# GpSimd forms the inverses of the softmax sums itself, with a power of minus one, in place of VectorE's reciprocals

## The chip, the core and the metric

The kernel runs on one core of one Trainium2 chip. The metric is the device time of one launch in microseconds (us), the median of three runs. A core has TensorE (PE in the profile, its weight loads apart as PEld), VectorE (DVE), ScalarE (ACT), GpSimd (POOL) and SyncE (SP, which here only issues DMAs).

## What is computed

A transformer layer in float32: layernorm, attention with 16 heads and a relative position bias, residual; then layernorm and a mixture of 16 experts, of which each token takes four.

```python
q = split_heads(hidden_states @ Wq)      # k and v likewise; B=8, S=512, d_model=128, 16 heads of 64
scores = einsum('bhqd,bhkd->bhqk', q, k) + compute_bias(rel_bias, S, S)
attn = softmax(scores, axis=-1)
ctx = einsum('bhqk,bhkd->bhqd', attn, v)
x = x + ctx.transpose(0, 2, 1, 3).reshape(B, S, -1) @ Wo
topv, topi = top_k(logits(layernorm(x)), 4)
x = x + sum_k softmax(topv)[k] * expert[topi[k]](layernorm(x))
```

## The kernel before

Every engine has its own program, written out by hand, and semaphores tie them together. The attention is a loop over the batch number `b` (0 to 7, 512 tokens each) and, in it, the head pair `i` (0 to 7): 64 steps, here called pairs. Each pair has four visits `v`, one for each 128 rows of queries, and each visit has two heads `hh`, so that a pair has eight score tiles of 128x512.

A tile passes through the engines in this order. TensorE forms the scores (`scores`, L1334, three products of split operands). VectorE adds the bias, writes the tile to `prob` in SBUF, and takes the row's extreme into `nmax` (`scores`, L1040, semaphore `neg_rdy`). ScalarE takes the exponential in place and accumulates the row's sum into `rsum` (`exps`, L884, `exp_rdy`). VectorE inverts the two sums of a visit in one instruction of 128x2 (`reciprocal`, L1046, `rinv_rdy`). GpSimd multiplies both tiles of the visit by the inverses (`normalise_probs`, L816, `norm_rdy`). After that the visits part. Tiles of visits 0 and 1 are transposed in blocks by VectorE (`turn_blocks`, L1062, `tr_rdy`), written to DRAM and read back as `pt_d`, and TensorE weighs the values with them one pair later (`weigh_early`, L1403). Tiles of visits 2 and 3 are transposed by TensorE one pair later (`weights_t`, L1348), copied by ScalarE to `pt_e` (L890) and used by `weigh_late` (L1387). TensorE's order in a pair is: scores of four visits, transposes of the pair before (L1348) with the output projection (L1414) between them, projections of the next pair (L1285 to L1287), `weigh_late`, `weigh_early`.

`weigh_late` waits for `neg_rdy` of the seventh tile of the pair in hand, (3,0), because its bank is shared. On VectorE the tile (3,0) stands behind `turn_blocks(b, i, 0)`, and that waits for `norm_rdy` of visit 0. The order on VectorE is `step` at L1215: four score tiles, reciprocal 0, two tiles, `turn_blocks` 0, tile (3,0), reciprocal 1, tile (3,1), the low parts of the next pair's queries and keys (L1023, L1018), `turn_blocks` 1, reciprocals 2 and 3.

GpSimd's program in the loop (`step` at L819) has, besides the four visits, some work for the routing of the batch before: a power of minus a half on 128x4 for each of the two layernorms (L808, L345), copies, one small multiplication (L348), and the scatters of the routed tokens, one indirect DMA (L372) of 128 rows each, 16 for a batch. They come behind the visits that this table names:

```python
ROUTE_POOL = {(2, 1): ("rstd",), (3, 2): ("copy",), (5, 3): ("weights",)}
SCATTER_AT = [(5, 0), (5, 1)] + [(i, v) for i in (6, 7, 8, 9) for v in range(3)] + [(10, 0), (10, 1)]
LAST_SCATTERS = [(i, v) for i in (5, 6) for v in range(TC)] + [(7, 0)]
```

An `i` of 8 to 10 is pair 0 to 2 of the next batch. So from pair 5 to pair 2 of the next batch the six pairs carry 2, 3, 3, 3, 3 and 2 scatters, in six of the batches; pairs 3 and 4 carry none, and the last batch has four in each of pairs 5 and 6. Ahead of the ninth and the thirteenth scatter of a batch a small copy (L368) is made that the scatter waits for. Behind the attention, the experts' blocks run (L1469 to L1494); the change touches nothing there.

Of the kernel before, what the change touches and what calls it, by code (L numbers as in the profile page):

```python
# [25 lines left out]
ALU = mybir.AluOpType  # L26
# [3 lines left out]
P = 128  # L30
# [7 lines left out]
def layer_kernel(nc, x, wq, wk, wv, wo, rel_bias, onehot, ident, expert_no, before_tok, region, home_row, pad,  # L38
# [17 lines left out]
    TILES = 2 * TC  # L56
    CHUNKS = NPR * TILES
# [28 lines left out]
    with ExitStack() as ctx:  # L86
        def sb(name, shape, dt=F32, stack=ctx):
            return stack.enter_context(nc.sbuf_tensor(name, shape, dt))

        def sem(name):  # L90
            return ctx.enter_context(nc.semaphore(name))
# [2 lines left out]
        x_all = sb("x_all", [P, NCH, D])  # L94
        idn = sb("idn", [P, P])
        minus_half = sb("minus_half", [P, TC])
        stats = sb("stats", [P, 2, TC, 6])
        moments = sb("moments", [P, 2, TC, 2])
        var_eps = sb("var_eps", [P, 2, TC])
# [64 lines left out]
        rsum = sb("rsum", [P, TILES], stack=attn)  # L164
        rinv = sb("rinv", [P, TILES], stack=attn)
# [32 lines left out]
        half_rdy = sem("half_rdy")  # L198
# [4 lines left out]
        s_rdy, neg_rdy, exp_rdy, rinv_rdy, norm_rdy = (sem(n) for n in  # L203
                                                       ("s_rdy", "neg_rdy", "exp_rdy", "rinv_rdy", "norm_rdy"))
# [62 lines left out]
        def pair_after(b, i, k):  # L267

            return divmod(b * NPR + i + k, NPR)
# [35 lines left out]
        def goes_on(b):  # L305

            return b <= LAST
# [490 lines left out]
        def _(pool):  # L798
# [1 line left out]
            pool.memset(done[:], 0.0).then_inc(no_done, 1)  # L800
            pool.memset(ones[:], 1.0).then_inc(one_rdy, 1)
            pool.memset(ones_bf[:], 1.0).then_inc(one_rdy, 1)
            pool.wait_ge(half_rdy, 1)

            def rsqrt(n):

# [2 lines left out]

            def normalise_probs(b, i, v):  # L810

                pool.wait_ge(rinv_rdy, b * VISITS + i * TC + v + 1)
                pool.nop(nofuse=True)
                for hh in range(2):
                    tile = prob[:, v, hh, :]
                    pool.tensor_scalar(tile, tile, rinv[:, 2 * v + hh:2 * v + hh + 1], 1.0, ALU.mult, ALU.mult)\  # L816
                        .then_inc(norm_rdy, 1)
# [192 lines left out]
        def _(dve):  # L1010
# [29 lines left out]
                dve.tensor_tensor_reduce(prob[:, v, hh, :], score_bank(v, hh)[:], strips[:, 2 * i + hh, v * P:v * P + S],  # L1040
                                         -1.0, BIG, ALU.add, ALU.min, nmax[:, n:n + 1]).then_inc(neg_rdy, 1)

            def reciprocal(b, i, v):

                dve.wait_ge(exp_rdy, b * CHUNKS + TILES * i + 2 * v + 2)
                dve.reciprocal(rinv[:, 2 * v:2 * v + 2], rsum[:, 2 * v:2 * v + 2]).then_inc(rinv_rdy, 1)  # L1046

            def turn_blocks(b, i, v):

                if (b, i) == (LAST, NPR - 1):  # L1050
# [59 lines left out]
            def early_extras(b, i):  # L1110

                if i == NPR - 2 and b < LAST:
                    normalise(dve, b + 1, 0, xn, rstd_rdy, xn_rdy)
                if i == 3 and exists(b - 1):
                    route_dve(dve, b - 1, 3)
# [99 lines left out]
            def step(b, i):  # L1215
                up = pair_after(b, i, 1)
                scores(b, i, 0, 0)
                scores(b, i, 0, 1)
                scores(b, i, 1, 0)
                scores(b, i, 1, 1)  # L1220
                reciprocal(b, i, 0)
                scores(b, i, 2, 0)
                scores(b, i, 2, 1)
                turn_blocks(b, i, 0)
                early_extras(b, i)
                scores(b, i, 3, 0)
                reciprocal(b, i, 1)
                scores(b, i, 3, 1)
                extras(b, i)
                if goes_on(up[0]):  # L1230
                    queries_lo(*up, queries_bank)
                    keys_lo(*up, keys_bank)
                if i == NPR - 2 and b < LAST:
                    tokens_lo(b + 1)
                turn_blocks(b, i, 1)
                reciprocal(b, i, 2)
                late_extras(b, i)
                reciprocal(b, i, 3)

            def drain():  # L1240
                turned_lo(0, 0)
# [448 lines left out]
```

## Time and profile before

| what | value |
|---|---|
| device time, median of 3 runs | 1121.62 us (1121.6 to 1124.82) |
| profiled execution, first to last instruction (span) | 1087.2 us |
| device time of the profiled execution by itself | not listed; the median of the runs stands 34.4 us above the span |
| TensorE busy | 1056.9 us, 97% of the span |
| VectorE busy | 834.8 us, 77% |
| ScalarE busy | 839.7 us, 77% |
| GpSimd busy | 685.9 us, 63% |
| mean granted TensorE clock | 0.990 |

"Busy" is the time in which an instruction of that engine was at work. The attention takes about the first 780 us of the span. The page divides the span into 40 slices of 27 us, and in those of the attention, but for the first and the last, GpSimd's share is between 4 and 7 tenths.

### The profile page before, as it was taken

The page shows a single profiled execution, that of the slowest core. Times are in us where ns is not written, and L with a number is a line of the kernel's source. Part 1 is how long each engine was busy: PE and PEld are TensorE (multiplying, and loading weights), DVE is VectorE, ACT ScalarE, POOL GpSimd, SP SyncE. Part 2 cuts the span into 40 slices and gives each one's busy share as a digit, 9 for nine tenths or more (in the row PEclk, how much of TensorE's full clock was granted, in tenths as well). Part 3 has the DMA queues.
Part 4 walks back from the last instruction along what each step waited for, and adds up shares of the span by engine and source line. Part 5 has one row for each costly group of instructions (what it writes and reads, how often), then busy time and mean ns, then how long its engine had stood idle before and what let it go on. Part 6 is the DMA issues. An engine that isn't in the chain of part 4 may idle for free.

```text
span 1087.2 us, 27487 instructions
## 1 busy us (share of the span) xinstructions
PE 1056.9 (97%) x8509; PEld 863.7 (79%) x8510; DVE 834.8 (77%) x2568; ACT 839.7 (77%) x2050; POOL 685.9 (63%) x890
## 2 busy tenths in 40 slices
PE   8999999999999999999999999999799999999993
PEld 4777777777777777777777777777599999999993
DVE  6877888888888978988898888888546444457775
ACT  5888888888888888888888888878667666777661
POOL 4654556774776568477657756665756777655553
PEclk9999999999999999999999999999999999999997
DMA  7676666776676677576757666787722623234552
GB/s 212 177 198 192 194 172 181 206 210 171 207 208 184 179 198 208 165 222 194 201 163 216 194 174 194 207 261 227 252 66 82 158 70 105 79 95 133 162 174 69
DMA packets 135344, 189.09 MB, mean 174 GB/s; under 512 B 19000, under 2 KB 108608, under 8 KB 135216
## 3 DMA queue, kind: packets, MB, share of 16 engines
q1 hardware_dynamic: 126064, 170.65, 55.5%
q0 software_dynamic: 9152, 16.88, 4.6%
q8 instruction: 63, 1.03, 0.4%
q14 instruction: 65, 0.53, 0.2%
HBM read 101.18 MB, written 88.23 MB: 174 GB/s over the span
## 4 chain that ended last, share of the span: by engine, by line
PE 80%; DMA 6%; DVE 5%; issue 4%; POOL 2%; SPq 1%; ACT 1%; DVEq 0%; POOLq 0%; ACTq 0%
PE bank L1334 14%; PE bank L1494 13%; PE bank L1403 9%; PE bank L1348 8%; PE bank L1387 8%; PE bank L1414 4%; PE bank L1481 3%; PE bank L1483 3%; PE bank L1482 3%; PE bank L1285 3%; PE bank L1287 3%; PE bank L1286 3%; DMA pt_d<-pt_dram 3%; DVE shared L1040 2%; DMA pt_dram<-turned 2%
## 5 line engine op out<-in xcount | busy, mean ns | idle before, releaser
L816 POOL TENSOR_SCALAR shared<-shared,rinv 128x512 f32<-128x512 f32 x512 | 351.8, 699 | 224.9 <-DVE rinv L1046 222.9
L884 ACT ACTIVATE shared<-shared,nmax 128x512 f32<-128x512 f32 x512 | 368.4, 733 | 75.8 <-DVE nmax L1040 75.8
L1040 DVE CUSTOM_DVE_ANT_0 shared<-bank,shared 128x512 f32<-128x512 f32 x512 | 330.1, 682 | 77.6 <-issue 33.1
L851 POOL DMA_INDIRECT y_dram<-yb,home x158 | 162.0, 1026 | 94.0 <-issue 47.6
L372 POOL DMA_INDIRECT xs_dram<-copies,slot x128 | 134.8, 1053 | 62.0 <-issue 48.9
L1062 DVE STREAM_TRANSPOSE turned<-shared 128x512 f32<-128x512 f32 x248 | 161.0, 687 | 10.7 <-issue 10.7
L890 ACT ACTIVATE pt_e<-bank 128x512 f32<-128x512 f32 x256 | 145.1, 596 | 18.0 <-PE bank L1348 17.2
L1494 PE MATMUL bank<-shared,act_h 128*128 x1264 | 154.1, 275 | 1.3 <-DVE yb L1188 0.7
L1494 PEld LDWEIGHTS bank<-shared,act_h 128*128 128x128 f32 x1264 | 148.0, 192 | 1.9 <-issue 1.9
L1348 PE MATMUL bank<-idn,shared 128*128 128x128 f32 x1024 | 136.6, 276 | 0.5 <-DVE nmax L1040 0.5
L1348 PEld LDWEIGHTS bank<-idn,shared 128*128 128x128 f32 x1024 | 112.8, 141 | 24.1 <-issue 12.7
L1387 PE MATMUL bank<-pt_e,v_sb 128*64 128x256 f32 x1024 | 124.6, 385 | 3.5 <-DVE nmax L1040 3.0
L916 ACT ACTIVATE act_h<-bank,shared 128x256 f32<-128x256 f32 x316 | 124.2, 476 | 3.4 <-PE bank L1483 3.2
L1403 PE MATMUL bank<-pt_d,v_sb 128*64 128x256 f32 x1008 | 122.7, 385 | 3.8 <-DMA pt_d<-pt_dram 3.5
L1387 PEld LDWEIGHTS bank<-pt_e,v_sb 128*64 128x64 f32 x1024 | 71.1, 136 | 49.2 <-issue 23.6
L1334 PE MATMUL bank<-k_hi,q_lo 64*128 64x512 f32 x512 | 109.1, 421 | 0.9 <-DVE q_lo L1023 0.6
L884 ACT ACTIVATION_READ_ACCUMULATOR shared<-shared,nmax 128x1 f32 x512 | 106.6, 208 | 0.0
L1403 PEld LDWEIGHTS bank<-pt_d,v_sb 128*64 128x64 f32 x1008 | 73.6, 138 | 38.3 <-issue 7.9
L1334 PE MATMUL bank<-k_hi,q_hi 64*128 64x512 f32 x512 | 101.0, 388 | 0.0
L1334 PE MATMUL bank<-k_lo,q_hi 64*128 64x512 f32 x512 | 100.9, 388 | 0.0
L1481 PE MATMUL bank<-xbt_hi,w_lo 128*128 128x256 f32 x316 | 95.6, 303 | 0.0
L1188 DVE TENSOR_TENSOR yb<-bank,shared 128x256 f32<-128x256 f32 x79 | 33.5, 424 | 79.9 <-PE bank L1494 79.9
(162 smaller groups left out, 1886.7 us busy)
## 6 DMA issues: line engine op xcount, KB each, us to landing
pt_dram<-turned SPq DMA_DIRECT2D x496, 128.0 KB
pt_d<-pt_dram SPq DMA_DIRECT2D x124, 512.0 KB
xb<-xs_dram SPq DMA_DIRECT2D x79, 129.0 KB, 2.9
shared<-in_experts SPq DMA_DIRECT2D x16, 514.0 KB
shared<-y_dram SPq DMA_DIRECT2D x32, 256.0 KB, 4.6
shared<-roll_dram SPq DMA_DIRECT2D x4, 768.0 KB, 8.2
y_dram<-yb,home POOLq DMA_INDIRECT x158
xs_dram<-pad_sb SPq DMA_DIRECT2D x17, 129.0 KB, 2.2
```

Of the source, the lines that this page charges most:

```text
L372: pool.indirect_dma_start(xs_dram, bass.IndirectOffsetOnAxis(ap=slot[:, c * TOP + k:c * TOP + k + 1], axis=0), copies[:, c, k % 2, :], Non ...
L816: pool.tensor_scalar(tile, tile, rinv[:, 2 * v + hh:2 * v + hh + 1], 1.0, ALU.mult, ALU.mult)\
L851: pool.indirect_dma_start(y_dram, bass.IndirectOffsetOnAxis(ap=home[:, j, c:c + 1], axis=0), yb[:, j, c, :], None, bounds_check=last_row, ...
L884: act.activation(prob[:, v, hh, :], prob[:, v, hh, :], ACT.Exp, bias=nmax[:, n:n + 1], scale=-1.0, accum_out=rsum[:, n:n + 1]).then_inc(ex ...
L890: act.activation(pt_e[:, hh, :, (v - 2) * P:(v - 1) * P], weights_bank(b, i, v, hh)[:].rearrange("p (j q) -> p j q", j=TC), ACT.Copy)\
L1040: dve.tensor_tensor_reduce(prob[:, v, hh, :], score_bank(v, hh)[:], strips[:, 2 * i + hh, v * P:v * P + S], -1.0, BIG, ALU.add, ALU.min, n ...
L1062: dve.transpose(turned[:, v, :, :, hh, :].rearrange("p k j r -> p j k r"), prob[:, v, hh, :].rearrange("p (j k c) -> p j k c", k=TC, c=BK) ...
L1334: mm = pe.matmul(score_bank(v, hh)[:], q[rows, i % 2, v * P:(v + 1) * P], k[rows, i % 2, :], start=(m == 0), stop=(m == 2))
L1348: mm = pe.transpose(weights_bank(b, i, v, hh)[:, j * P:(j + 1) * P], prob[:, v, hh, j * P:(j + 1) * P], idn[:])
L1387: pe.matmul(ps_a[DH * hh:DH * hh + DH, 2 * P:4 * P], v_sb[:, i // 2 % 2, j, col:col + DH], pt_e[:, hh, j, :], start=(j == 0), stop=(j == T ...
L1403: mm = pe.matmul(ps_a[DH * hh:DH * hh + DH, 0:2 * P], v_sb[:, i // 2 % 2, j, col:col + DH], src[:, :, :, j, hh, :].rearrange("p v a r -> p ...
L1494: mm = pe.matmul(ps_y[:, c * D:(c + 1) * D], act_h[:, q % 2, f, c * P:(c + 1) * P], params[:, bass.ds(w + (W2 + f * D), D)], start=(f == 0 ...
```

## The change

GpSimd no longer waits for VectorE's reciprocal. In each visit it waits for the exponentials of the visit, raises the two sums to the power of minus one, waits for its own result, and normalises as before. VectorE's 256 reciprocals are gone. A tile `minus_one` of 128x2 is set once at the start.

```diff
+        minus_one = sb("minus_one", [P, 2])
...
-            pool.wait_ge(half_rdy, 1)
+            pool.memset(minus_one[:], -1.0).then_inc(half_rdy, 1)
+            pool.wait_ge(half_rdy, 2)
...
             def normalise_probs(b, i, v):
 
+                pool.wait_ge(exp_rdy, b * CHUNKS + TILES * i + 2 * v + 2)
+                pool.nop(nofuse=True)
+                pool.tensor_tensor(rinv[:, 2 * v:2 * v + 2], rsum[:, 2 * v:2 * v + 2], minus_one[:], ALU.pow).then_inc(rinv_rdy, 1)
                 pool.wait_ge(rinv_rdy, b * VISITS + i * TC + v + 1)
                 pool.nop(nofuse=True)
                 for hh in range(2):
...
-            def reciprocal(b, i, v):
-
-                dve.wait_ge(exp_rdy, b * CHUNKS + TILES * i + 2 * v + 2)
-                dve.reciprocal(rinv[:, 2 * v:2 * v + 2], rsum[:, 2 * v:2 * v + 2]).then_inc(rinv_rdy, 1)
-
...
                 scores(b, i, 1, 1)
-                reciprocal(b, i, 0)
                 scores(b, i, 2, 0)
...
                 scores(b, i, 3, 0)
-                reciprocal(b, i, 1)
                 scores(b, i, 3, 1)
...
                 turn_blocks(b, i, 1)
-                reciprocal(b, i, 2)
                 late_extras(b, i)
-                reciprocal(b, i, 3)
```

On GpSimd, in a pair with three scatters (`shared` holds `prob`), the order of instructions before was

```order
L816 TENSOR_SCALAR shared<-shared,rinv 128x512 x4
L368 COPY copies<-home_sb 128x4
L372 DMA xs_dram<-copies,slot 69888x129
L816 TENSOR_SCALAR shared<-shared,rinv 128x512 x2
L372 DMA xs_dram<-copies,slot 69888x129
L816 TENSOR_SCALAR shared<-shared,rinv 128x512 x2
L372 DMA xs_dram<-copies,slot 69888x129
```

and with the change it is

```order
L816 TENSOR_TENSOR rinv<-rsum,minus_one 128x2
L821 TENSOR_SCALAR shared<-shared,rinv 128x512 x2
L816 TENSOR_TENSOR rinv<-rsum,minus_one 128x2
L821 TENSOR_SCALAR shared<-shared,rinv 128x512 x2
L369 COPY copies<-home_sb 128x4
L373 DMA xs_dram<-copies,slot 69888x129
L816 TENSOR_TENSOR rinv<-rsum,minus_one 128x2
L821 TENSOR_SCALAR shared<-shared,rinv 128x512 x2
L373 DMA xs_dram<-copies,slot 69888x129
```

One power stands ahead of every two multiplications; nothing else on GpSimd changed its place, and each power stands behind the scatter of the visit before.

On VectorE, at the end of a pair and the start of the next, the order before, with the semaphores that each waits for, was

```order
L1062 STREAM_TRANSPOSE turned<-shared 128x4x4x32 [waits norm_rdy]
L1046 RECIPROCAL rinv<-rsum 128x2 [waits exp_rdy]
L436 TENSOR_REDUCE esum<-ev 128x4 [waits ev_rdy]
L439 RECIPROCAL einv<-esum 128x4 [waits es_rdy]
L1046 RECIPROCAL rinv<-rsum 128x2 [waits exp_rdy]
L1040 ISA shared,nmax<-bank,shared 128x512 [waits tr_rdy,s_rdy]
```

and with the change it is

```order
L1062 STREAM_TRANSPOSE turned<-shared 128x4x4x32 [waits norm_rdy]
L437 TENSOR_REDUCE esum<-ev 128x4 [waits ev_rdy]
L440 RECIPROCAL einv<-esum 128x4 [waits es_rdy]
L1045 ISA shared,nmax<-bank,shared 128x512 [waits tr_rdy,s_rdy]
```

The reciprocals of visits 2 and 3 stood behind the transposes of visit 1; with the change nothing of VectorE stands between ScalarE's sums and GpSimd.

## Rows read from the trace of the kernel before

**Rows 1.** The page, its first part: busy us (share of the span) xinstructions.

```profile
PE 1056.9 (97%) x8509; PEld 863.7 (79%) x8510; DVE 834.8 (77%) x2568; ACT 839.7 (77%) x2050; POOL 685.9 (63%) x890
```

**Rows 2.** Windows: us, busy of PE, PEld, DVE, ACT, POOL, clock, DMA share, GB/s.

```profile
454.84:525.12 70.28, 70.14 (x558) 53.58 (x556) 59.95 (x188) 59.69 (x146) 51.40 (x68) 1.00 0.71 204
479.00:525.12 46.12, 46.12 (x370) 35.18 (x368) 38.72 (x121) 39.40 (x96) 35.57 (x47) 1.00 0.74 213
525.12:550.44 25.32, 25.19 (x204) 19.17 (x203) 22.23 (x74) 20.18 (x49) 12.57 (x19) 1.00 0.60 167
743.44:768.58 25.14, 23.46 (x188) 18.14 (x186) 19.79 (x62) 19.79 (x49) 18.25 (x24) 1.00 0.78 233
```

**Rows 3.** Waits: engine line <- releaser: us in total, times, longest us.

```profile
POOL shared L816 <- DVE rinv L1046: 222.9, 149, 4.5
```

**Rows 4.** Timeline of TensorE, pair 1 of batch 4: start, us, engine, line.

```profile
406.51 0.50 PE L1334 MATMUL bank<-k_hi,q_lo 64*128 64x512 f32 x2
...
414.41 1.95 PE L1387 MATMUL bank<-pt_e,v_sb 128*64 128x256 f32 x16
...
418.01 0.50 PE L1334 MATMUL bank<-k_hi,q_lo 64*128 64x512 f32 x2
```

**Rows 5.** Timeline of VectorE, the same pair.

```profile
411.95 1.30 DVE L1062 STREAM_TRANSPOSE turned<-shared 128x512 f32<-128x512 f32 x2
413.18 0.65 DVE L1040 CUSTOM_DVE_ANT_0 shared<-bank,shared 128x512 f32<-128x512 f32 x1
```

**Rows 6.** Timeline of GpSimd, the same pair.

```profile
407.11 1.37 POOL L816 TENSOR_SCALAR shared<-shared,rinv 128x512 f32<-128x512 f32 x2 [1.93 <-DVE rinv L1046]
408.65 1.05 POOL L372 DMA_INDIRECT xs_dram<-copies,slot  x1 [0.17 <-issue]
409.74 2.70 POOL L816 TENSOR_SCALAR shared<-shared,rinv 128x512 f32<-128x512 f32 x4
```

**Rows 7.** Timeline of ScalarE: the sums of tiles (2,1), (3,1), then (0,1).

```profile
404.73 0.24 ACT L884 ACTIVATION_READ_ACCUMULATOR shared<-shared,nmax 128x1 f32 x1
...
406.14 0.23 ACT L884 ACTIVATION_READ_ACCUMULATOR shared<-shared,nmax 128x1 f32 x1
...
409.67 0.19 ACT L884 ACTIVATION_READ_ACCUMULATOR shared<-shared,nmax 128x1 f32 x1
```

**Rows 8.** Groups of instructions: xcount | busy us, mean ns of one | idle before.

```profile
L345 POOL TENSOR_TENSOR rstd<-var_eps,minus_half 128x4 f32<-128x4 f32 x8 | 8.4, 1056 | 0.8 <-DVE var_eps L387 0.6
L808 POOL TENSOR_TENSOR rstd<-var_eps,minus_half 128x4 f32<-128x4 f32 x8 | 8.2, 1024 | 4.6 <-DVE var_eps L387 4.6
L368 POOL COPY copies<-home_sb 128x4 f32<-128x4 f32 x16 | 3.1, 191 | 0.0
L348 POOL TENSOR_TENSOR wt<-ev,einv 128x16 f32<-128x16 f32 x8 | 1.7, 212 | 0.0
L1046 DVE RECIPROCAL rinv<-rsum 128x2 f32<-128x2 f32 x256 | 36.4, 148 | 0.3
```

**Rows 9.** Timeline: hand-overs to GpSimd from a result just made.

```profile
425.27 0.17 DVE L1046 RECIPROCAL rinv<-rsum 128x2 f32<-128x2 f32 x1
...
425.61 0.69 POOL L816 TENSOR_SCALAR shared<-shared,rinv 128x512 f32<-128x512 f32 x1 [1.00 <-DVE rinv L1046]
...
496.82 1.06 POOL L372 DMA_INDIRECT xs_dram<-copies,slot  x1 [0.78 <-POOL copies L368]
...
1030.93 0.42 DVE L1188 TENSOR_TENSOR yb<-bank,shared 128x256 f32<-128x256 f32 x1 [0.43 <-PE bank L1494]
...
1032.10 0.97 POOL L851 DMA_INDIRECT y_dram<-yb,home  x1 [1.09 <-DVE yb L1188]
```

**Rows 10.** Timeline, last batch, pair 6, four scatters: GpSimd, VectorE, TensorE.

```profile
762.10 1.37 POOL L816 TENSOR_SCALAR shared<-shared,rinv 128x512 f32<-128x512 f32 x2
...
762.88 1.33 DVE L1062 STREAM_TRANSPOSE turned<-shared 128x512 f32<-128x512 f32 x2 [1.96 <-issue]
...
764.95 1.95 PE L1387 MATMUL bank<-pt_e,v_sb 128*64 128x256 f32 x16 [1.45 <-DVE nmax L1040]
```

## The prediction

> **What bounds the kernel now.** The page's first part comes first [rows 1]: TensorE is busy for 97% of the span, GpSimd for 63%. By these shares GpSimd has room to spare. The shares are averages over stages, though, and the change puts work on GpSimd in the attention alone, so I looked there by windows [rows 2]. The first row is a stretch from pair 5 of batch 4 to pair 2 of batch 5, from the start of one pair's scores on TensorE to another's: six pairs in 70.28 us, with the 16 scatters of a batch. TensorE is busy for 70.14 of it at full granted clock (1.00), so it sets the pace: some 11.5 us for a pair, as from 406.51 to 418.01 [rows 4]. GpSimd is busy for 51.40. The row from 525.12 is the two pairs without scatters behind it: GpSimd is busy for 12.57 of 25.32. So GpSimd's load is uneven, and what the change costs must be read in the stretches with scatters.
>
> The view of waits then shows GpSimd idle for 222.9 us, in 149 waits for VectorE's inverse [rows 3]. It reads like a loss that the change takes back. It is mostly spare time: the engine that sets the pace doesn't wait for it.
>
> **Whether a late GpSimd is felt.** The normalised tiles of visit 0 are wanted first. In the pair of [rows 4 to 6] GpSimd normalises the last visit of the pair before and visit 0 from 409.74 to 412.44 without a break; VectorE transposes from 411.95 to 413.25, scores tile (3,0) from 413.18 to 413.83, and TensorE starts `weigh_late`, which waits for that tile, at 414.41. That leaves 0.5 us. The last batch shows what happens beyond it [rows 10]: in a pair with four scatters the normalising of visit 0 starts only at 762.10, VectorE idles 1.96 us before its transposes, and TensorE then idles 1.45 us, its wait put down to VectorE. The window from 743.44, two such pairs, has TensorE busy for only 23.46 of 25.14 us [rows 2]. So where GpSimd's work for a pair is longer than the pair, the pair grows to GpSimd's time. This limit exists already, and the change loads the engine that has it.
>
> **What goes.** 256 reciprocals of 148 ns [rows 8], 36.4 us of VectorE's time. VectorE is busy for 59.95 of 70.28 us in the stretch and TensorE hardly waits for it, so I set this at nothing; a gain is bounded by the 0.14 us in which TensorE is idle in the stretch. The wait also goes in which GpSimd's work on visits 2 and 3 stood behind VectorE's transposes of visit 1: tile (2,1) was summed at 404.97, tile (3,1) at 406.37 [rows 7], and GpSimd started at 407.11 after 1.93 us idle [rows 6]. It can now start at 405. This is real, and it is why I may count GpSimd as a queue that runs without holes when it is late.
>
> **What comes.** In each of 256 visits a power of 128x2 and a wait of GpSimd for its own result. Call their sum x.
>
> The trace has no power of 128x2. One of 128x4 takes 1.02 to 1.06 us, while a copy of the same 128x4 takes 0.19 [rows 8]. So the power itself adds 0.83. If that goes by elements, two columns cost 0.19 + 0.42 = 0.6 us; if it goes by the instruction, 1.02. These are my inner bounds. The outer one below is 0.2, that of any small instruction: a multiplication of 128x16 takes 0.21. I take 0.6: that multiplication with four times the columns costs the same as the copy, so what the power adds seems to be work done per element and not per instruction. The row can't prove it.
>
> The wait: VectorE's reciprocal ends at 425.44 and GpSimd starts at 425.61, 0.17 us later [rows 9]. A scatter behind a copy starts 0.78 us after it, which would be 0.6 more; but a scatter behind VectorE's result (ended 1031.35, started 1032.10) also takes 0.75, so the extra belongs to the indirect DMA and not to waiting for oneself. I take 0.15 and keep 0.78 as the bound above.
>
> So x is 0.75, by the other reading of the power 1.17; the ends are 0.35 and 1.8 (1.02 and 0.78).
>
> **The sum.** First the point from which it decides. In the stretch GpSimd is busy for 51.40 us; beside it stand 14 gaps of 0.17 before scatters [rows 6] and two of 0.78 behind copies [rows 9], 3.9 us. 70.3 less 55.3 leaves 15.0 us for 24 visits: x up to 0.62 fits. In the two pairs behind, 8 visits have 25.32 - 12.57 = 12.7 us, 1.6 a visit, so they are hit only near the upper end.
>
> By pairs, at x = 0.75: two normalisings take 1.35 (2.70 for four), and with a scatter behind them 2.63 (407.11 to 409.74) [rows 6]; a visit then takes 2.10 or 3.38. Pair 5 needs 11.2 us and pair 6 12.2, which fits. Pair 7 needs 12.2, pairs 0 and 1 need 13.0 each (with the small copy and its gap, 0.8), pair 2 12.0 (with a power of 1.02). Together 50.3 us, where there are now 46.12, the row from 479.00 to 525.12 [rows 2]: 4.2 over. GpSimd may be late by some 1.0 us first: visit 0's sums are ready at 409.86 [rows 7], so its tiles can be done at 411.96 instead of 412.44, and there was 0.5 us left. So 3.2 us for each stretch, and there are six: 19. The two pairs with four scatters need 8 x 3.38 + 0.2 = 27.2 us against 25.14: 2.1 over, less 1.0, makes 1. The first pair, where all wait for the first tiles, 0.5. At the end of the attention visits 2 and 3 are released sooner; nothing. Sum: 20.5 us on the 1087.2 of the profiled execution. The median of the runs is 34.4 us above that span, outside of what the profile shows, and I leave this part as it is: 1121.6 + 20.5 = **1142**.
>
> The memset and the tile `minus_one` cost 0.1 us while the input loads; nothing.
>
> **The rivals.**
>
> *The power is cheap: no change.* x = 0.35. GpSimd needs 55.3 + 8.4 = 63.7 of 70.28 us in the stretch; no pair without four scatters is late. In the pairs with four, 27.2 - 3.2 = 24.0 of 25.14 us are needed, and visits 2 and 3 start sooner, so that up to the 1.45 us of [rows 10] comes back in each. 1119 to 1122. For it: the reciprocal on VectorE is as cheap as that, and small instructions cost 0.2. Against it: both powers in the trace cost five times that. It decides from x below 0.65. Chance 0.14, of which 0.03 for over 0.3% faster.
>
> *The power costs by the instruction.* x = 1.17; visits take 2.52 and 3.80 us. Pairs 5 to 2 then need 12.8, 13.9, 13.9, 14.7, 14.7 and 13.7, together 83.7 against 70.3: 13.4 over, less 0.5 that may be late, 13.0; six make 78. The pairs with four scatters add 5, the start 1: 84 us, 1206. For it: the same 1.02 in all 16 powers, with no second size. Against it: the argument on the elements above. Values of x between the two lie between 1142 and 1206. Chance 0.28, with these.
>
> *The wait for oneself is dear.* With 0.78 and a power of 1.02, a visit takes 3.15 without a scatter, four of them 12.6 us, over the 11.5 us of every pair. Each stretch gives 13.4 + 24 x 0.61 = 28, the six 168, and the other 28 pairs about 1 each: some 200 us, 1320. With a power of 0.6 x is 1.38 and the time about 1240. Chance 0.05.
>
> **How the numbers follow.** The forecast, slower by GpSimd's excess at x near 0.75, has 0.53, with 1128 to 1158 as its own range (x 0.68 to 0.85). The range leaves out the cheap power and the dear wait, 0.19 in all, and reaches from the lower end of the forecast to just above the costly power: 1127 to 1209. A measurement of this kernel can tell about 0.3%, 3.4 us, from no change. Faster 0.03, same 0.12, slower 0.85.
>
> **What would show it.** In the profile of the changed kernel the power of 128x2 stands in a row of its own: about 0.6 us if right. GpSimd's busy time rises by 256 times that, about 154 us, to some 840, and VectorE's falls by 36. Pairs with scatters are longer than 11.5 us, those from 7 to 2 most; VectorE waits for GpSimd's tiles before its transposes (L1062), and TensorE for VectorE before `weigh_late` (L1387). Pairs 3 and 4 keep their 25.3 us. The prediction is wrong in size if the power's row says 1.0, wrong in kind if pairs without scatters grow too, and wrong in sign if the six pairs still take 70.3 us.

## The result, and the profile after

The changed kernel takes 1201.07 us (median of 4 runs, 1198.94 to 1207.33) against 1121.61 for the kernel before (4 runs, 1119.62 to 1124.82): a ratio of 1.0703 [1.0679, 1.0728], 79.5 us more. The forecast of 1142 had the direction right and the size wrong by a factor of four; the time lies inside the range, which reaches up to the 1206 us of the dear power, a rival that did not come true.

Of the changed kernel, the page's first part and, from the groups of instructions of GpSimd, the three that matter (busy us, mean ns | idle before):

```profile
PE 1096.0 (91%) x8509; PEld 887.3 (74%) x8510; DVE 822.9 (69%) x2312; ACT 844.0 (70%) x2050; POOL 885.0 (74%) x1147
```

```profile
L821 POOL TENSOR_SCALAR shared<-shared,rinv 128x512 f32<-128x512 f32 x512 | 349.7, 694 | 44.5 <-POOL rinv L816 44.5
L816 POOL TENSOR_TENSOR rinv<-rsum,minus_one 128x2 f32<-128x2 f32 x256 | 184.5, 721 | 80.9 <-ACT shared L889 77.5
L373 POOL DMA_INDIRECT xs_dram<-copies,slot x128 | 139.7, 1091 | 58.8 <-issue 47.7
```

The power costs 0.72 us and the wait for it 44.5 / 256 = 0.17. So x is 0.89, where the prediction took 0.75. GpSimd's busy time rose by 199 us [rows 1], the 222.9 us of waits for VectorE's inverses [rows 3] are gone, and TensorE went from 97% busy to 91% (96% in a second trace of the kernel before, which is used from here on; its span is 1120.6 us).

The chain that ended last, by engine, says who sets the pace now. TensorE had 80% of it in the first trace of the kernel before, GpSimd 2%.

```profile
PE 50%; POOL 25%; issue 12%; ACT 4%; DVE 4%; DMA 3%; another core or an unknown queue 0%; SPq 0%; POOLq 0%; DVEq 0%; ACTq 0%
```

The stretch of [rows 2] again, at its times in this trace, and the two pairs behind it (windows: us, busy of PE, PEld, DVE, ACT, POOL, clock, DMA share, GB/s):

```profile
497.80:577.06 79.26, 72.28 (x560) 55.30 (x558) 58.80 (x162) 60.21 (x146) 66.71 (x90) 1.00 0.66 180
577.06:604.42 27.36, 25.32 (x204) 19.11 (x203) 23.01 (x68) 20.29 (x49) 20.47 (x31) 1.00 0.57 157
```

70.28 became 79.26, and the two pairs that were to keep their 25.3 us became 27.36. A pair's period is the time from the start of its scores on TensorE to the start of the next pair's. Periods in us in batch 5, pairs 5 to 7, and batch 6, pairs 0 to 4 (before: the second trace):

| pair | 5 | 6 | 7 | 0 | 1 | 2 | 3 | 4 |
|---|---|---|---|---|---|---|---|---|
| before | 11.50 | 12.31 | 12.07 | 11.50 | 11.51 | 11.51 | 13.25 | 12.07 |
| after | 11.50 | 15.67 | 11.77 | 12.94 | 13.69 | 13.69 | 17.16 | 11.92 |

Summed over all: the six stretches from pair 5 to pair 2 give 51.4 us, pairs 3 and 4 of seven batches 21.0, the pairs up to batch 1's pair 2 give 4.8, and pairs 5 and 6 of the last batch 5.3. That is 82.5 in the attention (753.8 to 836.3 from the first scores to the last pair's), and the rest of the span is 2.7 shorter.

**Pairs 1 and 2: GpSimd is the bound.** GpSimd in pair 1 of the same stretch, a queue without holes but for the fixed short ones in brackets:

```profile
549.10 1.10 POOL L373 DMA_INDIRECT xs_dram<-copies,slot  x1 [0.18 <-issue]
550.24 0.73 POOL L816 TENSOR_TENSOR rinv<-rsum,minus_one 128x2 f32<-128x2 f32 x1
551.14 1.36 POOL L821 TENSOR_SCALAR shared<-shared,rinv 128x512 f32<-128x512 f32 x2 [0.17 <-POOL rinv L816]
552.68 1.10 POOL L373 DMA_INDIRECT xs_dram<-copies,slot  x1 [0.18 <-issue]
...
561.80 0.18 POOL L369 COPY copies<-home_sb 128x4 f32<-128x4 f32 x1
562.77 1.11 POOL L373 DMA_INDIRECT xs_dram<-copies,slot  x1 [0.79 <-POOL copies L369]
```

A visit with a scatter takes 3.58 us from scatter to scatter (549.10 to 552.68), and a pair has three; a visit without one is 2.23; the copy and its gap cost 0.7 more. Together 13.7, which is the pair's period. This part went as the prediction has it.

**Pair 6: GpSimd starts late.** The end of pair 5 and pair 6, on GpSimd, on VectorE and on TensorE:

```profile
507.17 1.11 POOL L373 DMA_INDIRECT xs_dram<-copies,slot  x1 [3.63 <-issue]
...
517.38 1.37 POOL L821 TENSOR_SCALAR shared<-shared,rinv 128x512 f32<-128x512 f32 x2 [0.17 <-POOL rinv L816]
```

```profile
506.21 0.18 DVE L460 CAST slot<-slotf 128x16 int32<-128x16 f32 x1
...
518.16 1.33 DVE L1062 STREAM_TRANSPOSE turned<-shared 128x512 f32<-128x512 f32 x2 [1.80 <-issue]
519.42 1.20 DVE L393 TENSOR_SCALAR xt<-x_all,moments,rstd 128x128 f32<-128x128 f32 x4
```

```profile
520.77 0.63 PE L1275 MATMUL bank<-idn,xt 128*128 128x128 f32 x4 [1.57 <-DVE xt L393]
521.38 1.95 PE L1383 MATMUL bank<-pt_e,v_sb 128*64 128x256 f32 x16
```

The first scatter of a batch, at (5,0), needs the slots (L460), which VectorE computes late in pair 5. GpSimd idles 3.63 us for them, with three visits of pair 5 queued behind; it starts 0.78 us after they are done (0.77 in the kernel before). The three visits and visit 0 of pair 6 then run back to back and end at 518.75, 11.6 us behind the scatter's start. In the kernel before it is 8.0 (464.26 to 472.30); the 3.5 between them are four times x. VectorE's transposes of visit 0 wait for that. Behind them stands `xt`, the normalised tokens (L393), and TensorE waits for `xt`, not for the score tile behind it (two shorter waits, of 0.67 and 0.25 us, stand earlier in the pair). In the trace of before the same wait of the scatter is there, and VectorE's transposes begin at 471.98 without a gap. GpSimd and VectorE there:

```profile
464.26 1.11 POOL L372 DMA_INDIRECT xs_dram<-copies,slot  x1 [4.19 <-issue]
```

```profile
471.98 1.30 DVE L1062 STREAM_TRANSPOSE turned<-shared 128x512 f32<-128x512 f32 x2
473.20 1.08 DVE L392 TENSOR_SCALAR xt<-x_all,moments,rstd 128x128 f32<-128x128 f32 x4
```

TensorE takes up `xt` at 474.43, 0.15 us after it is done: the slack that the prediction counted on was already used up.

**Pair 3: three things at once.** VectorE and TensorE in pair 3 of batch 4:

```profile
475.64 1.33 DVE L1062 STREAM_TRANSPOSE turned<-shared 128x512 f32<-128x512 f32 x2 [1.35 <-issue]
476.89 1.86 DVE L393 TENSOR_SCALAR copies<-x_all,moments,rstd 128x128 f32<-128x128 f32 x4
```

```profile
478.90 0.63 PE L323 MATMUL bank<-idn,copies 128*128 128x128 f32 x4 [2.05 <-DVE copies L393]
479.51 3.54 PE L1383 MATMUL bank<-pt_e,v_sb 128*64 128x256 f32 x16
```

VectorE waits 1.35 us for late tiles. Its four copies take 1.86, though the same four took 1.08 before (at 436.20, with GpSimd idle). TensorE, idle for 2.05, then takes 3.54 for sixteen matmuls that take 1.95 elsewhere (above, 521.38). The granted clock shows why:

```profile
476.00:478.00 2.00, 0.85 (x4) 0.37 (x2) 2.00 (x5) 2.00 (x5) 1.83 (x4) 1.00 0.40 146
478.00:480.00 2.00, 1.10 (x8) 0.87 (x10) 2.00 (x7) 0.46 (x2) 1.41 (x2) 0.93 0.95 233
480.00:482.00 2.00, 2.00 (x13) 1.38 (x12) 2.00 (x4) 2.00 (x6) 0.82 (x2) 0.50 0.05 12
482.00:484.00 2.00, 2.00 (x14) 1.24 (x10) 0.39 (x1) 0.27 (x2) 2.00 (x5) 0.72 0.34 74
```

After two windows in which TensorE was busy for about half, the clock is at 0.50, the lower of its two levels. It is partly there so in the windows beside it (0.93 and 0.72). Four of the seven pairs 3 are like that (three of 17.1 us, one of 18.73 with a longer fall); two without the drop take 15.48, and batch 1's, with no scatters of a batch before, 14.11. So a fall costs 1.6 us, and those of pair 3 make 8.2 of the 21.0. The clock fell twice more in the attention of this execution, in its first pair and in pair 6 of the last batch; at 1.6 each, falls make about 11 of the 82.5 us (an estimate: seven times 1.6, the longer one counted twice). In both traces of the kernel before the clock is at 1.00 in all 64 pairs.

### The profile page after: what moved, and what is told of

Its sections match the earlier page's. It is cut to its first block, busy times and chain, and to the rows that moved or that the text cites. A ratio compares the mean times of both kernels' runs of the same rounds, so it can differ in the third digit from the quotient of the medians.

```text
span 1200.4 us, 27744 instructions
## 1 busy us (share of the span) xinstructions
PE 1096.0 (91%) x8509; PEld 887.3 (74%) x8510; DVE 822.9 (69%) x2312; ACT 844.0 (70%) x2050; POOL 885.0 (74%) x1147
## 4 chain that ended last, share of the span: by engine, by line
PE 50%; POOL 25%; issue 12%; ACT 4%; DVE 4%; DMA 3%; another core or an unknown queue 0%; SPq 0%; POOLq 0%; DVEq 0%; ACTq 0%
PE bank L1490 13%; POOL shared L821 10%; POOL rinv L816 7%; PE bank L1330 7%; POOL xs_dram L373 6%; PE bank L1383 6%; PE bank L1399 5%; PE bank L1344 3%; PE bank L1477 3%; PE bank L1479 3%; PE bank L1478 3%; ACT shared L889 2%; PE bank L1410 1%; PE bank L1465 1%; PE bank L1281 1%
## 5 line engine op out<-in xcount | busy, mean ns | idle before, releaser
L889 ACT ACTIVATE shared<-shared,nmax 128x512 f32<-128x512 f32 x512 | 367.2, 727 | 83.5 <-DVE nmax L1045 73.6
L1045 DVE CUSTOM_DVE_ANT_0 shared<-bank,shared 128x512 f32<-128x512 f32 x512 | 326.4, 684 | 95.0 <-issue 52.5
L821 POOL TENSOR_SCALAR shared<-shared,rinv 128x512 f32<-128x512 f32 x512 | 349.7, 694 | 44.5 <-POOL rinv L816 44.5
L856 POOL DMA_INDIRECT y_dram<-yb,home x158 | 175.2, 1109 | 110.5 <-issue 75.9
L816 POOL TENSOR_TENSOR rinv<-rsum,minus_one 128x2 f32<-128x2 f32 x256 | 184.5, 721 | 80.9 <-ACT shared L889 77.5
L1062 DVE STREAM_TRANSPOSE turned<-shared 128x512 f32<-128x512 f32 x248 | 161.8, 690 | 80.4 <-issue 79.5
L373 POOL DMA_INDIRECT xs_dram<-copies,slot x128 | 139.7, 1091 | 58.8 <-issue 47.7
L1490 PE MATMUL bank<-shared,act_h 128*128 x1264 | 161.9, 283 | 15.7 <-DVE yb L1188 5.9
L1490 PEld LDWEIGHTS bank<-shared,act_h 128*128 128x128 f32 x1264 | 151.6, 196 | 22.7 <-issue 22.5
L1344 PE MATMUL bank<-idn,shared 128*128 128x128 f32 x1024 | 145.2, 279 | 13.1 <-POOL shared L821 11.8
L1383 PE MATMUL bank<-pt_e,v_sb 128*64 128x256 f32 x1024 | 131.7, 401 | 20.9 <-DVE nmax L1045 15.6
L1383 PEld LDWEIGHTS bank<-pt_e,v_sb 128*64 128x64 f32 x1024 | 79.4, 141 | 65.4 <-issue 42.9
L1399 PEld LDWEIGHTS bank<-pt_d,v_sb 128*64 128x64 f32 x1008 | 78.8, 139 | 31.6 <-issue 5.8
```

Source lines behind the costliest of these rows:

```text
L373: pool.indirect_dma_start(xs_dram, bass.IndirectOffsetOnAxis(ap=slot[:, c * TOP + k:c * TOP + k + 1], axis=0), copies[:, c, k % 2, :], Non ...
L816: pool.tensor_tensor(rinv[:, 2 * v:2 * v + 2], rsum[:, 2 * v:2 * v + 2], minus_one[:], ALU.pow).then_inc(rinv_rdy, 1)
L856: pool.indirect_dma_start(y_dram, bass.IndirectOffsetOnAxis(ap=home[:, j, c:c + 1], axis=0), yb[:, j, c, :], None, bounds_check=last_row, ...
L889: act.activation(prob[:, v, hh, :], prob[:, v, hh, :], ACT.Exp, bias=nmax[:, n:n + 1], scale=-1.0, accum_out=rsum[:, n:n + 1]).then_inc(ex ...
L1062: dve.transpose(turned[:, v, :, :, hh, :].rearrange("p k j r -> p j k r"), prob[:, v, hh, :].rearrange("p (j k c) -> p j k c", k=TC, c=BK) ...
L1344: mm = pe.transpose(weights_bank(b, i, v, hh)[:, j * P:(j + 1) * P], prob[:, v, hh, j * P:(j + 1) * P], idn[:])
```

## The experiments

After the measurement above, the kernels ran in three series. The kernel before took 1126 us in the first, 1088 in the second and 1123 in the third. The difference lies in the expert blocks behind the attention (about 350 us against 318), not in the attention. What makes it isn't shown: the record gives chip 13 for the first series and chip 1 for both others. So each kernel is compared with the kernel before in its own series, by the ratio and by the difference, and pairs are compared by their periods.

**The kernel before and the changed one once more.**

> The kernel before, unchanged, for one more profile. The first profile of it has a span of 1087.2 us beside run times of 1121.6, while the changed kernel's span (1200.4) lies 1.9 us under its time. If the 34 us lie outside of the span, this span is again near 1087 with a time near 1121. If the first profile was only a quicker execution, this one has a span within 3 us of its time. Either way the 64 pairs of the attention should take 754 us from the first scores to those of the last pair, as in the first profile; what differs should lie in the experts' blocks.

> The changed kernel once more, beside the others of this call. 1201 us, ratio 1.070; attention 836 us from the first scores to those of the last pair (before: 754).

Measured: before 1122.54 with a span of 1120.6, 753.8 us in the attention (the first trace has 754.0). The changed kernel 1200.39, ratio 1.0687 [1.0648, 1.0726]. The result repeats. Its attention does not to the microsecond: 830.0 us where 836 was expected. The six stretches give 51.4 again and the last batch's pairs 5.3, but pairs 3 and 4 give 17.9 for 21.0, since the clock fell in three pairs 3 (batches 3, 5 and 7) and not in four, and the start 1.6 for 4.8. So 76 to 82 us is what the attention lost, and which pairs 3 have the fall changes from one execution to the next. The 34.4 us that stood between the median and the first trace's span were no time outside the profile: the expert blocks take 318 us in the first trace and 350 in this one.

**What a power costs by its size.** At the end of the kernel before, three powers of each size:

```diff
+            for n in (1, 2, 4, 8, 16):
+                for _ in range(3):
+                    pool.tensor_tensor(pw_out[:, at_col:at_col + n], pw_in[:, 0:n], pw_ex[:, 0:n], ALU.pow)
+                    at_col += n
```

> The kernel before with powers of minus one of 128x1, x2, x4, x8 and x16, three of each, at the very end of GpSimd's program. With 0.72 us for two columns and 1.02 for four in the kernels, a straight line gives 0.15 us a column on 0.42: 0.57, 0.72, 1.02, 1.6 and 2.8 us. If the cost went in steps of four columns, 1, 2 and 4 columns would cost the same, which the two sizes already speak against unless the exponent matters (minus one here, minus a half there).

```profile
L869 POOL TENSOR_TENSOR pw_out<-pw_in,pw_ex 128x16 f32<-128x16 f32 x3 | 8.6, 2896 | 0.0
L869 POOL TENSOR_TENSOR pw_out<-pw_in,pw_ex 128x8 f32<-128x8 f32 x3 | 4.8, 1632 | 0.0
L869 POOL TENSOR_TENSOR pw_out<-pw_in,pw_ex 128x4 f32<-128x4 f32 x3 | 3.0, 1021 | 0.0
L869 POOL TENSOR_TENSOR pw_out<-pw_in,pw_ex 128x1 f32<-128x1 f32 x3 | 2.4, 811 | 0.1
L869 POOL TENSOR_TENSOR pw_out<-pw_in,pw_ex 128x2 f32<-128x2 f32 x3 | 2.0, 688 | 0.0
```

From two to sixteen columns (2.896 - 0.688) / 14 = 0.158 us a column, which leaves 0.37 for none; four and eight columns fit (1.00 and 1.63). One column doesn't by its mean of 0.81, but of the three the very first takes 1.35 and the others 0.55 and 0.54, beside 0.53 by the line; why the first is long isn't shown. The price does go by elements, but on a foot of 0.37 and not of the copy's 0.19. Hence 0.69 and not 0.60.

**A multiplication in place of the power.** The tiles are then not divided by their sums.

```diff
-                pool.tensor_tensor(rinv[:, 2 * v:2 * v + 2], rsum[:, 2 * v:2 * v + 2], minus_one[:], ALU.pow).then_inc(rinv_rdy, 1)
+                pool.tensor_tensor(rinv[:, 2 * v:2 * v + 2], rsum[:, 2 * v:2 * v + 2], minus_one[:], ALU.mult).then_inc(rinv_rdy, 1)
```

> The power is replaced by a multiplication of the same two columns (so the tiles are not normalised); both waits stay. Theory: what counts is GpSimd's time for a visit; the multiplication takes 0.2 us where the power takes 0.72, so x falls from 0.89 to 0.37, GpSimd needs some 64 of the 70.3 us of six pairs with scatters, and the time is within 0.5% of before, 1118 to 1128. Rival: the wait of GpSimd for its own result, or the wait for ScalarE in place of VectorE, is what costs; then most of the 80 us stays, 1170 or more.

Measured: 1136.67, ratio 1.0112 [1.0078, 1.0146]. x is 0.37 here, so five sixths of the cost go with 0.52 us of power a visit. But 1118 to 1128 was expected, the prediction's first rival had no change at this x, and 12.6 us remain: pair 3 takes 14.1 us in every batch from 1 on (14.0 in one) though GpSimd idles 138 us for ScalarE, and pair 6 takes 13.5 (6.9 us over six of them). The copies of the tokens (L393) take 520 ns each for 340 before.

**The same with GpSimd's visits held** until VectorE has made the score tiles ahead of the old place of its reciprocal (for visits 2 and 3 these are all eight; their reciprocals had stood behind the transposes of visit 1 too):

```diff
+                if (b, i) != (LAST, NPR - 1):
+                    pool.wait_ge(neg_rdy, TILES * (b * NPR + i) + (4, 7, 8, 8)[v])
+                    pool.nop(nofuse=True)
```

> The changed kernel with a multiplication in place of the power (the tiles are divided by no sum: they are multiplied by minus the sum), and each visit of GpSimd held until VectorE has reached the place where its reciprocal stood before. Without the hold this kernel took 1.1% over the kernel before (1136.67 us), with VectorE's copies of the turned tokens at 0.52 us each for 0.34. If it is the time at which GpSimd now works beside VectorE's copies that makes them slow, the hold brings them back to 0.34, pair 3 from 14.1 to 13.3 us and the whole to 1124 to 1128. If GpSimd's 0.37 us in each visit is the cause, it stays at 1136 or goes to 1145.

Measured: 1091.88 against 1088.12, ratio 1.0040 [1.0019, 1.0061]. More waiting took away two thirds of the remainder, as expected if the copies are what costs. VectorE and GpSimd in pair 3 of batch 1, first without the hold, then with it:

```profile
150.26 1.93 DVE L393 TENSOR_SCALAR copies<-x_all,moments,rstd 128x128 f32<-128x128 f32 x4
```

```profile
150.24 1.36 POOL L821 TENSOR_SCALAR shared<-shared,rinv 128x512 f32<-128x512 f32 x2 [0.17 <-POOL rinv L816]
```

```profile
150.05 1.08 DVE L393 TENSOR_SCALAR copies<-x_all,moments,rstd 128x128 f32<-128x128 f32 x4
```

```profile
147.57 1.36 POOL L824 TENSOR_SCALAR shared<-shared,rinv 128x512 f32<-128x512 f32 x2 [0.17 <-POOL rinv L819]
151.94 0.19 POOL L819 TENSOR_TENSOR rinv<-rsum,minus_one 128x2 f32<-128x2 f32 x1 [3.00 <-DVE nmax L1048]
```

Without the hold GpSimd normalises from 150.24 to 151.60, beside the copies, and they take 1.93; with it GpSimd is idle, and they take 1.08. The first two of the four copies carry all of it:

```profile
150.26 1.42 DVE L393 TENSOR_SCALAR copies<-x_all,moments,rstd 128x128 f32<-128x128 f32 x2
```

In the trace's single records they take 0.75 and 0.76 us, and each ends 0.08 us behind the end of one of GpSimd's two multiplications (150.93 and 151.60). The last two take 0.34 each, as with GpSimd idle, though GpSimd's power of 128x4 runs beside them from 151.56 to 152.58. Pair 3 is back at 13.25. The old wait for VectorE's reciprocal kept the two engines apart at this place, though the program has it for the data alone. What is left is pair 6: it takes 13.5 us, 6.7 more over six of them, while other pairs give some back. By the rows that is the late scatter with four visits of 0.37 behind it; no run tested it at this x.

**VectorE's reciprocals kept**, into a tile that nothing reads.

```diff
+            def reciprocal(b, i, v):
...
+                dve.reciprocal(rinv_copy[:, 2 * v:2 * v + 2], rsum[:, 2 * v:2 * v + 2]).then_inc(copy_done, 1)
```

> The changed kernel, with VectorE's reciprocals kept at their old places, written to a tile that nothing reads. The change took some 36 us of busy time off VectorE. If that freed nothing that the end waits for, this is 1200 again, within 3 us. If it saved a part of the cost, it is 1205 to 1215.

Measured: 1163.42 against 1088.12, ratio 1.0701 [1.0660, 1.0742], that of the change itself. Ridding VectorE of 36 us of work bought nothing.

**The power beside the reciprocals:** the kernel before, with a power ahead of GpSimd's wait for VectorE.

```diff
+                pool.tensor_tensor(idle_pow[:], ones[:, 0:2], minus_half[:, 0:2], ALU.pow).then_inc(idle_rdy, 1)
                 pool.wait_ge(rinv_rdy, b * VISITS + i * TC + v + 1)
```

> The kernel before, VectorE's reciprocals kept and used, with a power of 128x2 on GpSimd ahead of each visit's wait for the reciprocals; its result goes into a tile that nothing reads. It tells what GpSimd's time alone costs, without the dependence. If that time is all, a visit takes 0.69 to 0.75 us more, and 60 to 85% of the 80 us of the change come back: 1170 to 1190. If the dependence (sum, then power, then tiles) is what costs, it stays under 1140, since the power here can run while GpSimd would wait.

Measured: 1133.29 against 1088.12, ratio 1.0408 [1.0381, 1.0435]: 45 us, 57% of the change's 79.5 (60% of the 75 that the kernel above costs in the same series). That is just under or at the lower end of what the theory of GpSimd's time gave and far over the other. Pairs 1 and 2 take 13.0 us for 13.69: 0.7 less, which is four waits of 0.17. The copies take 339 ns, and pair 3 14.0 us. So GpSimd's 0.72 us alone cost over half. The rest, by the traces: the six stretches lose 36.7 us here for 51.4, pairs 3 and 4 4.5 for 21.0 (17.9 in the second trace), and the clock falls nowhere in this attention. With the order of VectorE's reciprocals the slow copies and the falls are gone too. How much of the rest is the wait of 0.17 by itself this run doesn't tell.

**The first two scatters one visit later**, in the changed kernel:

```diff
-        SCATTER_AT = [(5, 0), (5, 1)] + [(i, v) for i in (6, 7, 8, 9) for v in range(3)] + [(10, 0), (10, 1)]
+        SCATTER_AT = [(5, 1), (5, 2)] + [(i, v) for i in (6, 7, 8, 9) for v in range(3)] + [(10, 0), (10, 1)]
```

> The changed kernel, with the first two scatters of a batch one visit later: at (5,1) and (5,2) in place of (5,0) and (5,1). If pair 6 is late because the first scatter waits for VectorE's slots and the visits left behind it each carry the power and its wait (0.89 us), then only three visits of pair 5 and pair 6's first stand behind it no longer: visit 0 of pair 5 is done before, and pair 6 (15.7 us in the changed kernel) falls by one visit's 2.2 to 2.7 us; over six stretches 13 to 16 us of the change's 80 come back, 1184 to 1188. If the whole sum of GpSimd's work in the queue decides (the theory of the prediction), nothing is gained: the same tiles and scatters stand in the queue up to pair 2, and it is 1200 again, with pair 6 shorter and pair 0 longer by the same amount.

Measured: 1153.96 against 1088.12, ratio 1.0592 [1.0559, 1.0625]. In the same series the kernel with the reciprocals kept, which costs what the change costs, takes 1163.42: 9.5 us came back, or 12 by the two ratios. The six stretches, which the expectation is about, lose 38.2 us for 51.4, 13 less; a fourth fall of the clock in pairs 3, for three, hides some of it. The slots are ready as before, and the scatter starts 0.78 us behind them, but one visit more is done by then:

```profile
598.30 0.18 DVE L460 CAST slot<-slotf 128x16 int32<-128x16 f32 x1
```

```profile
599.26 1.11 POOL L373 DMA_INDIRECT xs_dram<-copies,slot  x1 [0.85 <-issue]
```

Pair 6 takes 13.46 for 15.67, and pairs 1 and 2 keep 13.69. So the late start was a cost of its own, and the theory by which the whole sum of GpSimd's work decides, so that nothing would be gained, is refuted.

**And visit 1 of pair 3 held as well:**

```diff
+                if i == 3 and v == 1:
+                    pool.wait_ge(neg_rdy, TILES * (b * NPR + i) + 7)
+                    pool.nop(nofuse=True)
```

> The changed kernel with its first two scatters one visit later (1.0592 in its own run) and, in pair 3 alone, visit 1 of GpSimd held until VectorE has made the seventh tile of scores, as VectorE's reciprocal held it before. If the copies of the turned tokens (512 ns for 340) are slow because GpSimd works beside them, they are back at 0.34 and pair 3 is 0.8 us shorter in the seven batches: 1.054. If in pair 3 it is rather the queue's lateness that sets the time, the copies are faster but the held visit makes GpSimd later by up to 1.5 us, and the whole is 1.059 or over.

Measured: 1180.33 against 1123.12, ratio 1.0505 [1.0471, 1.0539]. 1.7 times the gain that was expected. The copies are back at 337 ns, and pair 3 takes 14.7 us in five batches and 15.0 in one, where without the hold it takes 15.49 in two and 17.1 in four. TensorE idles 1.26 us before the copies' transposes for 2.04, and the clock falls in no pair 3. Pairs 3 and 4 lose 7.6 us over seven batches, for 19.3. The periods separate the two parts: 15.49 to 14.70 are the copies, 0.8 in each batch, and 15.49 to 17.1 is a fall of the clock, 1.6 in each of four.

**The power of the next visit ahead of a scatter**, in the changed kernel, so that the scatter covers the wait for it:

```diff
                     for n, q in scatters_at(b, i, v):
+                        power(*((b, i, v + 1) if v + 1 < TC else (b, i + 1, 0) if i + 1 < NPR else (b + 1, 0, 0)))
                         route_pool(pool, n, q)
```

> The changed kernel, in which the power of the next visit stands ahead of a scatter and not behind it, wherever a scatter is due; the scatter (1.09 us) then covers the 0.17 us that GpSimd waited for its own power. 16 of the 24 visits of a stretch have a scatter, so up to 16 x 0.17 = 2.7 us of the queue go, 16 us over six stretches, and 1201 becomes 1185 (ratio to the kernel before 1.056). If the exponentials of the next visit aren't done so early, the scatter now waits for them, and half of that or nothing comes back: 1193 to 1201. If the wait for its own power is no part of the cost at all, and only the 0.72 us count, it stays at 1201 (1.070).

Measured: 1188.50 against 1123.12, ratio 1.0570 [1.0536, 1.0605]. Pairs 1 and 2 take 13.16 for 13.69, which is three waits of 0.17, as the first theory had it. That the total meets it too is luck. `xt` now meets GpSimd and takes 538 ns for 427, TensorE pauses for it, and the clock falls in five of the six pairs 6: they take 17.0 to 18.5 us, and the one without a fall 15.52, no more than before (15.67). So the six stretches together gain nothing, 51.2 for 51.4. Pair 6's pause is 2.47 us for 1.57. Pair 3's is 1.8 for 2.04, with a fall in one batch alone, and from batch 2 on it takes 15.2 in the others: pairs 3 and 4 lose 12.5 for 21.0. Most of the falls moved from pair 3 to pair 6.

**The change in pair 4 alone:**

```diff
+        OWN = (4,)
...
+                if i in OWN:
+                    return
                 dve.wait_ge(exp_rdy, b * CHUNKS + TILES * i + 2 * v + 2)
```

> The kernel before, with the change in pair 4 of each batch alone (32 of 256 visits): GpSimd forms the inverses there, VectorE in all other pairs. The queue has no scatter in pair 4, so by both theories the 4 x 0.89 = 3.6 us are covered: GpSimd waits 4.6 us or more for VectorE's inverses there. If that holds, no difference (ratio 0.998 to 1.002). If lateness of pair 4 reaches VectorE's slots and the first scatter, or if GpSimd's early visits slow VectorE's own copies (512 ns for 340 in the changed kernel, but those stand in pair 3), it shows as 0.2 to 0.5 us a pair, ratio up to 1.004.

Measured: 1123.64 against 1123.12, ratio 0.9994 [0.9973, 1.0015]. Where GpSimd has room and meets nobody, 0.89 us a visit are hidden. Pair 4 itself takes 11.9 us for 12.07 or more, too little to show in the time.

**The kernel before with the later scatters:**

```diff
-        LAST_SCATTERS = [(i, v) for i in (5, 6) for v in range(TC)] + [(7, 0)]
+        LAST_SCATTERS = [(5, v) for v in (1, 2, 3)] + [(6, v) for v in (0, 1, 2)] + [(7, 0)]
```

(and `SCATTER_AT` as above)

> The kernel before (VectorE's reciprocals) with its first two scatters one visit later and the last batch's seven scatters at (5,1) to (5,3), (6,0) to (6,2) and (7,0). Pair 6 is 12.3 to 12.7 us for 11.5 in the kernel before, and pair 6 of the last batch 13.2. If the first scatter's wait for VectorE's slots is what makes it so, some 0.5 us come back in each of six, and 1 us in the last: 3 to 4 us, ratio 0.997. If GpSimd's scatters then only end later, at pair 2, nothing: 1.000. The scatter moved behind visit 0 of pair 7 could cost 1 us there.

Measured: 1121.98 against 1123.12, ratio 0.9980 [0.9965, 0.9996]. Pair 6 falls to 12.10 from 12.3 to 12.8, and pairs 5 and 6 of the last batch together from 25.1 to 23.8. It is the one version whose interval lies below the kernel before, by 0.2%, less than the 0.3% that I would call a difference.

## Why the prediction was wrong in size

The direction and the engine were right: the change loads GpSimd, and pairs with scatters grow to its queue. Four terms of the sum failed. Of the 62 us that the attention lost beyond the forecast's 20.5, about 17 are x, 17 the late start and the slack in pair 6, 21 the pairs 3 and 4 that were set at nothing, and 7 the start and the last batch beyond that.

- **That GpSimd's queue decides once it fills the stretch, from x = 0.62: right as far as tested.** x = 0.37 costs 1% (for other reasons, above), x = 0.89 costs 7%, and pairs 1 and 2 take exactly what GpSimd's queue adds up to. No run has an x near 0.62.
- **"two columns cost 0.19 + 0.42 = 0.6 us": mis-sized.** 0.72 in the kernel (0.69 alone), since an instruction with a power has a foot of 0.37. The wait was taken at 0.15 and is 0.17. By the prediction's own sum x = 0.89 makes a visit 0.14 longer: pairs 5 to 2 need 73.6 + 24 x 0.14 = 77.0 for 70.3, less the 1.0 of lateness 5.7, over six stretches 34; with a unit more in the last batch and the start about 37, 1159. So this explains 17 of the 59 us that were missing.
- **"Pair 5 needs 11.2 us and pair 6 12.2, which fits": failed.** It took GpSimd's work as free to start when the sums are there. A scatter in the middle of pair 5 waits for VectorE's slots, and GpSimd can't use pair 5's spare time with it in front. The trace had the row (4.19 us of idle time at 464.26), and so had the view of waits, in the row `POOL xs_dram L372 <- issue: 48.9, 110, 4.3`. The prediction took the waits for the inverse alone from that view.
- **"GpSimd may be late by some 1.0 us first": failed.** The 0.5 us were read from pair 1 [rows 4, 5]. In pairs 3 and 6 the tokens' normalising stands between VectorE's transposes and TensorE, and the slack is nil. With the step before, this is 17 of the missing us (51.4 less 34); moving the scatter gave 13 back in the stretches.
- **"Pairs 3 and 4 keep their 25.3 us": failed**, 21 us. The queue is still late at pair 3; VectorE's copies are slow beside GpSimd (0.8 us a batch, 5.6); and in four pairs 3 the clock falls behind TensorE's pause (8.2). That leaves about 7 for the late queue. The copies and the clock can't be read off a sum of GpSimd's work, and the prediction has no term for either. The hold took both away, 12 us together.
- **"36.4 us of VectorE's time", set at nothing: right**, shown by keeping them.
- **The pairs with four scatters at 1 us and the start at 0.5: too small.** The first gave 5.3, again with the first scatter's wait (3.63 us, at 828.84) and the low clock; the start gave 4.8, and 1.6 in the second trace, where the clock didn't fall in the first pair.
- **"The median of the runs is 34.4 us above that span, outside of what the profile shows": wrong**, but it cancels. They were expert blocks that took less time in the profiled execution, and adding 20.5 to the median was the right thing to do.
- **Of the rivals**, the cheap power is refuted by the power's row, 0.72 us. The multiplication shows what it would have been worth: most of the cost goes, but not all, because of the copies and pair 6. The dear wait is refuted by 0.17. The power by the instruction had the right total at x = 1.17 for a wrong reason: its x is 0.3 too high, and the steps that it shares with the forecast are the ones that failed. The measured time lies in the range by the same luck: the range was stretched for that power, and the forecast's own went only to 1158.

## What to carry to other kernels

An engine with 37% idle time can still have none where the work is added. Count its queue in order, with the waits of other instructions in it, and find the instruction that can't start early: what stands behind it can't use the idle time ahead of it. Take the slack from the pair or stage that has the least. And when a wait is removed, look at which two engines it kept apart.

## What the hardware showed that was not expected

- **GpSimd's multiplications hold up VectorE's copies.** Four subtract-and-multiply copies of 128x128 on VectorE, from SBUF to SBUF, take 1.08 us with GpSimd idle and 1.93 beside two 128x512 multiplications of GpSimd, which keep their 1.36. VectorE's score tiles, which read PSUM, don't change (684 ns for 682). The Trainium skill (SBUF — State Buffer, SBUF: two separate sides) tells of one pair of ports that the two engines share as an exclusive lock, where the one that comes second is blocked for the whole instruction. The trace agrees where GpSimd multiplies: two copies start behind a multiplication, last 0.75 us for 0.34 and end 0.08 us behind its end. It does not agree for every instruction of GpSimd: beside a power of 128x4 (1.02 us) the copies take 0.34, as alone.
- **The granted clock fell after a pause of 2 us** to the lower of its two levels, and the next sixteen matmuls took 3.54 us for 1.95: 1.6 us for each fall. But in pair 3 of batch 5 a pause like it (2.04 us) left the clock at 1.00 (below), and in a second execution, with six pauses of 2.05 to 2.09, it fell in batches 3, 5 and 7 and not in the others. What decides between the two stays open. The window of that pause, columns as above:

```profile
585.00:587.00 2.00, 0.14 (x1) 0.00 (x0) 2.00 (x6) 1.31 (x3) 1.83 (x4) 1.00 0.45 108
```

- **A power on GpSimd** costs 0.37 us and 0.158 for each column of 128 elements; a multiplication of the same 128x2 costs 0.20.
- **The same kernel takes 1088 or 1122 us by the series.** The 34 us lie in one stage, the expert blocks, and next to nothing of them in the attention (753.8 and 754.0). The record names the same chip for a quick series and a slow one, so the cause is open.
